# Attention with a mixture of experts on one core: the weights' chunks and the routed rows' stores move from SyncE's DMA queue to ScalarE's

## The reference, cut to what matters

```
x = L0_attn_x                              # (2, 2048, 512), f32
xn = layernorm(x)
# attention: rmsnorm, ternary qkv weights, 16 heads of 32, chunks of 128 tokens
#   intra = (q k^T * decay mask) v ;  cross = q * decay * S ;  S = decay * S + k^T v
#   two rmsnorms of the result, ternary output projection
# ffn: router -> softmax -> top 2 of 8 experts, weights summed to one
#   routed = sum over the 2 experts of combine * (silu(x Wg) * (x Wu)) Wd      (256 wide)
#   shared = (silu(x Sg) * (x Su)) Sd                                           (1024 wide)
return x + attention(xn) + routed(xn) + shared(xn)
```

## Time and profile before

| | |
|---|---|
| median of 3 runs | 1262.44 us |
| the profiled execution | 1262.65 us |
| its span, first to last instruction | 1260.9 us |
| PE busy | 1200.6 us, 95% |
| DVE, ACT, POOL busy | 53%, 38%, 39% |
| mean granted TensorE clock | 0.992 |
| DMA moved | 217.4 MB, mean 172 GB/s |
| q1, the queue of SP | 180.03 MB |
| q10, the queue of ACT | 0.81 MB |

### The profile page before, as it was taken

How to read it: one execution, slowest core, us unless ns; L and a number is a source line. 1 busy time by engine, 2 the same in 40 slices (tenths; PEclk the granted TensorE clock), 3 DMA queues, 4 the chain that set the end, 5 groups by cost and what they waited for, 6 DMA issues and landing times. The chain is left out here.

```text
span 1260.9 us, 29255 instructions
## 1 busy us (share of the span) xinstructions
PE 1200.6 (95%) x10768; PEld 812.0 (64%) x10768; DVE 664.4 (53%) x1410; ACT 477.9 (38%) x1031; POOL 493.3 (39%) x432
## 2 busy tenths in 40 slices
PE   3899999999999779999999899999999999999998
PEld 3676677677677557777777444444444577777776
DVE  7998889898898578633333322222222233333333
ACT  6454555555555462322222233333333311111111
POOL 3366655665676210344410222222222044444443
PEclk9999999999999889999999999999999999999999
DMA  8388888788878674344432777788888544444443
GB/s 284 97 241 197 206 226 244 187 221 231 222 204 219 204 212 156 87 124 94 111 109 23 182 193 191 192 195 182 190 184 193 123 156 152 151 151 152 151 153 110
DMA packets 269373, 217.40 MB, mean 172 GB/s; under 512 B 196784, under 2 KB 203056, under 8 KB 269296
## 3 DMA queue, kind: packets, MB, share of 16 engines
q1 hardware_dynamic: 255344, 180.03, 54.3%
q0 software_dynamic: 12848, 35.47, 10.3%
q10 hardware_dynamic: 1104, 0.81, 0.2%
HBM read 115.97 MB, written 56.51 MB: 137 GB/s over the span
## 5 line engine op out<-in xcount | busy, mean ns | idle before, releaser
L596 PE MATMUL sc<-x,WG 128*128 128x256 f16 x3072 | 346.0, 273 | 0.3 <-PEq L2099 0.3
L596 PEld LDWEIGHTS sc<-x,WG 128*128 128x128 f16 x3072 | 300.6, 98 | 48.6 <-issue 0.8
L1609 PE MATMUL yp<-WD,work 128*128 128x512 f16 x768 | 176.2, 379 | 1.4 <-DVE work L2016 1.0
L1586 POOL DMA_INDIRECT raw<-xs_dram,slots x71 | 67.3, 948 | 280.2 <-DMA raw<-raw 127.0
L2011 DVE SCALAR_TENSOR_TENSOR work<-sc,up_inv,work 128x512 f32<-128x512 f32 x63 | 47.3, 750 | 244.4 <-ACT work L1844 244.2
L1844 ACT ACTIVATE work<-sc,gate_inv 128x512 f32<-128x512 f32 x63 | 43.3, 687 | 303.4 <-PE sc L596 299.9
L1609 PEld LDWEIGHTS yp<-WD,work 128*128 128x128 f16 x768 | 74.8, 98 | 79.8 <-DVE work L2016 2.3
L864 PE MATMUL ring<-WG 128*128 128x256 f16 x1024 | 120.9, 275 | 2.0 <-PEq L264 2.0
L2084 POOL DMA_INDIRECT raw<-y_dram,gidx x64 | 63.6, 994 | 130.3 <-DVE gidx L2000 113.2
L2221 DVE TENSOR_TENSOR work<-rat,work 128x256 f16<-128x256 f32 x71 | 30.1, 424 | 155.5 <-ACT work L2198 155.5
L1602 PE MATMUL sc<-WG,raw 128*128 x432 | 104.8, 379 | 6.6 <-PEq L1620 3.4
(11 more groups left out here) (263 smaller groups left out, 1749.7 us busy)
## 6 DMA issues: line engine op xcount, KB each, us to landing
y_dram<-raw SPq DMA_DIRECT2D x71, 256.0 KB
WD<-in_L_attn_x SPq DMA_DIRECT2D x16, 512.0 KB, 4.5
work<-in_L_ffn_w_gate_up SPq DMA_DIRECT2D x16, 512.0 KB, 4.7
xs_dram<-WG SPq DMA_DIRECT2D x16, 512.0 KB, 3.7
xT_dram<-x SPq DMA_DIRECT2D x16, 512.0 KB, 2.7
WG<-in_L_attn_x SPq DMA_DIRECT2D x16, 512.0 KB, 5.4
x_dram<-WG SPq DMA_DIRECT2D x32, 256.0 KB, 2.1
x<-xT_dram SPq DMA_DIRECT2D x16, 512.0 KB, 7.5
```

Source lines behind the costliest of these rows:

```text
L596: ins = pe.matmul(gu[:, h, f * 2 * P:(f + 1) * 2 * P].rearrange("p (u t) -> p u t", u=2), w[:, kk, b, part * P:(part + 1) * P], x[:, :, a ...
L1586: pool.indirect_dma_start(out=xg[:, r % XG], out_offset=None, in_=xs_dram, in_offset=bass.IndirectOffsetOnAxis(ap=slots[:, r, 0:1], axis=0 ...
L1609: ins = pe.matmul(y[:], act_hl[a][:, f, :], w[:, f, b, :] if len(w.shape) == 4 else w[:, 0, f, b, :], start=(first and f == 0 and (a, b) = ...
```

## The change

`load_weights` goes from SP's step to ACT's, where it stands after `x_high(*nxt)` and before `take_oT(0, ...)`. It keeps its wait in other words: the count passed is the chunk's own, two higher, so `n - 1` there is `n + 1` here. In the routed block the store of a tile's result goes from SP to ACT, where it stands after the `ah` copy of the next tile. SP keeps its wait on `gu_full` and the transposes there, and no longer waits for `y_ready`.

```
                 if front:
                     turn_x(*after(q, par))
                     store_xs(*after(q, par))
-                if norm:
-                    sp.wait_ge(S["wmax_ready"], n + 1)
-                    load_weights(q + 1, par)
-                elif front:
+                if front and not norm:
                     load_group(sp, k, 1)
...
+            def load_weights(q, par):
+
+                n = 2 * q + par
+                act.wait_ge(S["wmax_ready"], n - 1)
+                for w, size, a in zip(flat, PART, START):
+                    act.dma_start(wraw[:, par, a:a + size], w[:, bass.ds(n * size, size)]).then_inc(wraw_in[par], 16)
...
                 x_high(*nxt)
+                if norm:
+                    load_weights(q + 1, par)
                 take_oT(0, q, par, st)
...
                     for r in range(SLOT_TILES):
                         if XH <= r + 3 < SLOT_TILES:
                             wait_apart(sp, S["gu_full"], r + 3 - XH + 1, S["sp_passed"])
                             turn(sp, r + 3, S["sp_passed"])
-                        store(r)
...
+                    rows = y_dram.rearrange("(r p) c -> r p c", p=P)
+
+                    def store(q, par):
+                        r = 2 * q + par
+                        act.wait_ge(S["y_ready"], r + 1)
+                        act.dma_start(at_step(rows, r), ysb[:, par]).then_inc(y_out[par], 16)
...
+                        last = (q, 0) if par == 1 else (q - 1, 1)
                         if not first:
-                            y_evac(*((q, 0) if par == 1 else (q - 1, 1)))
+                            y_evac(*last)
                         act.wait_ge(S["at_full"], r + 1)
                         act.activation(ah[:, par], at[par][:], ACT.Copy).then_inc(S["ah_ready"], 1)
+                        if not first:
+                            store(*last)
 
                     run_steps(act, step)
                     y_evac(SLOT_TILES // 2, 0)
+                    store(SLOT_TILES // 2, 0)
```

More of the change, by code:

```diff
@@ L764, in store_x1 @@
                 sp.dma_start(dst[:, u], x1[:, u]).then_inc(x1_out[u], 16)
[L766 to L769, removed]
             def store_xT(q, par):
@@ L2125, in _ @@
                 def _(sp):
-                    rows = y_dram.rearrange("(r p) c -> r p c", p=P)
                     load_tokens(sp, 1, 0, HALF)
-                    def store(r):
-                        sp.wait_ge(S["y_ready"], r + 1)
-                        sp.dma_start(rows[r], ysb[:, r % 2]).then_inc(y_out[r % 2], 16)
                     for r in range(SLOT_TILES):
```

## The result

The changed kernel takes 1296.33 us (median of 4 runs, 1293.96 to 1300.87) against 1262.31 us before (4 runs, 1260.25 to 1265.57). The ratio is 1.0264, with a 95% interval of 1.0232 to 1.0296: 2.6% slower, and outside the range of 1255 to 1277.

A forecast was written before the change was run, and what follows sets the result against it. PE was taken to bound the kernel, with attention's steps sensitive to when `load_xl` lands. 1262.65 + 5.5 (attention's loop) - 3.3 (routed rows) = 1264.9 us, given as 1265, range 1255 to 1277.

The forecast's parts named there:

- The rule for the step: Attention's loop: a wait of `row_stats` for `load_xl` is free up to 0.66 us; beyond that it lengthens the step one for one.
- one lateness and not a sum: Attention: `turn_h` is delayed too, but gets no price of its own; PE's lateness from it and DVE is one by `proj(0)`.
- D: Attention: the delay in `load_xl`'s landing in every step from the earlier weights' chunk, taken as 0.7 us.
- the prediction's own sum: Attention's thirteen steps: waits lengthened by D give 13.5 us of excess where there were 8.05, so +5.5 us.
- The chunk moves about 8 us earlier: Attention: the weights' chunk is asked at 204.1 to 206.3, just ahead of `load_xl`, delaying it; net +5.5 us in the loop.
- my nearest row: Attention: `load_xr`, asked 0.5 us behind the chunk, lands after 5.4 us against 4.5 for `load_xl`, 0.9 us more.
- The 16% of idle share: Attention before `load_xl` lands: DMAs 84% busy; if the chunk fits into the idle 16%, D is 0.
- the chunk and everything else goes ahead: Attention, slower rival: all of it goes ahead of `load_xl`, D = 1.43, +15.0 us in the loop, 1274.4 us; chance 0.24.
- The highest bound: Attention: `load_xl` is delayed by the chunk's whole transfer time, 3.7 us, which gives +44 us.
- The wait for `wmax_ready` is ... past: ACT in attention: this wait is for a chunk read in the step before, so it costs 0.
- The relief of `turn_y`: Attention's loop: `turn_y` no longer lands late behind the weights' chunk and `load_xr`; 2.52 us counted as gained.
- The routed rows: Routed block: SP no longer waits for `y_ready`, so PE's two waits for a transpose should go, -3.3 us.

## Why the prediction was wrong

**The rule for the step** (a wait of `row_stats` over 0.66 us counts one for one) was right: 39.1 us by it, 39.2 measured. That `turn_h` and DVE are one lateness and not a sum was right for the changed kernel nearly to the end: PE waited 8.8 us for `turn_h` in three of the first steps, and the sum over the steps is explained without them, if by the luck of three errors that cancel. With DVE's wait shortened it was no longer free (26.4 us of such waits in the kernel with `row_stats` later). With D = 2.67 in the prediction's own sum the loop comes out at +31.1 us, as measured, so nothing but D was wrong in it.

**"The chunk moves about 8 us earlier", the term D** is the step that failed. It was taken as 0.7 us and was 2.67; times 13 this is 25.6 us of the 31 missed (1296.3 - 1265); 3.8 are step 0, below, and the median is 2.3 over the profiled execution. Three things in it were wrong.
- *The order.* I let ACT ask when `x_high` ends, about 204.1 in the step of the earlier trace rows, behind `turn_h` at 203.48. ACT's first issue comes 0.1 us after the first `x_high` starts (220.97 and 221.06), while its ACTIVATEs still run. So three of the chunk's four DMAs are asked ahead of `turn_h`. How much of D the order makes is not shown: held until `x_high` was done, 1.2 us later and behind the first transpose, the kernel was no faster.
- *Who is hit.* I counted the bytes ahead of `load_xl`'s landing and took the time of its ask as fixed. Per step the time from the start of `turn_h` to the ask of `load_xl` went from 3.96 to 6.07 us, from the ask to `row_stats` from 4.68 to 5.11 (means of thirteen steps). Of the delay of 2.5 us, 2.1 are SP held in the issue of two transposes. `load_xr`, my nearest row, stood right behind the chunk with no transpose between them, and could not show this.
- *The rate.* I used 322 GB/s, the rate of the earlier trace rows, from a stretch in which no transpose was issued. In the 13 us from the chunk's ask to `load_xl`'s landing the DMAs were busy throughout (1.08) and moved 267 GB/s; over the thirteen steps it is 273 on average, between 228 and 299. The 16% of idle share before was no spare room of 322 GB/s.

The rival "the chunk and everything else goes ahead" was right in kind, and its 1.43 us still too small, for the last two reasons. The highest bound, the chunk's whole time, 3.7 us, did hold D, but nothing between 1.43 and it was in the range.

**"The wait for `wmax_ready` is ... past"** failed in step 0: there ACT waits with the prologue's chunk not yet read, its four issues run from 58.39 to 60.87, and `take_oT(0)` follows late. Two rows of ACT's timeline:

```profile
59.88 0.99 ACTq L1128 DMA_DIRECT2D work<-in_L_ffn_w_sh_down  x1
60.92 0.60 ACT L1042 ACTIVATE WG<-ring 128x512 f32<-128x512 f32 x1 [4.98 <-issue]
```

It costs 3.8 us once, of which 3.3 are PE's wait for this eviction; the first stretch at the lower clock, at 63.3, lies behind it. The first `proj` is at 77.11 with a quarter of the bytes as well, but at 73.17 where ACT asks after `take_oT(1)`. In the other steps the issues cost nothing, as predicted: `take_oT(0)` starts at PE's release.

**The relief of `turn_y`** was right: PE waited 4.2 us for `yT` in the loop before, has no such wait in it after, and the 2.52 us are gone in the agreement of rule and excess. **The routed rows** were right: -3.3 us predicted, no wait for a transpose after, and about -3.7 us for that part alone, known to some 3 us.

Sum: 1262.65 + 31.1 (loop) + 3.8 (step 0) - 3.3 (routed) = 1294.3, beside 1293.99 of the profiled execution.

**Queue or moment.** Shown: the early moment costs 2.4% from SP and 2.6% from ACT. In the versions with a late transfer it is each time one in flight with the chunk (`turn_h` and `load_xl`, `turn_x`, or `turn_y(1)`); after `o_square(1)` it is ACT's own time for the issues. The Trainium skill ("DMA: Bandwidth & Descriptors", section "Issuing engines are not separate DMA queues") says that a second issuer saves only its sequencer's time; these runs agree: no version with the weights on ACT was faster than its like on SP (1.0264 beside 1.0244 early, 1.0004 beside 0.9965 late in the step), and the best one has them on SP. Open: how much the second queue adds by itself. In the early pair the transposes were held 2.1 us longer than before beside ACT's queue and 1.1 us longer behind the chunk on SP, but there the chunk was also 1 us further ahead of them. The other pair, ACT before `take_kv(1)` and SP behind `turn_y(1)`, is 0.4% apart with intervals that overlap, and their moments differ. Open too is why a transpose's issue takes longer beside a plain load; the runs show that it does, not what holds it.

## What to carry to other kernels

A transfer that is moved to another engine's queue also moves in time, and it loses its place in the one list that kept it behind the urgent ones; read the new moment from where that engine's DMA issues can start at the earliest, not from where its work before them ends. When a large load comes to lie beside transposes, price the issuing engine's held time and everything behind it in its list, and not only the bytes. If a load has slack, look for the stretch in which no transfer is waited for, and leave it on the queue whose order guarantees that stretch.

## What was unexpected of the hardware

- SP's issue of a DMA transpose (`turn_h`) took 1.24 us in the median before the change; with the weights in flight on the other queue it took 1.84 us and up to 4.0 (two of them 2.89 us and 5.04 in the mean). Its landing went from 3.1 to 6.2 us.
- ACT's DMA issues ran beside its own ACTIVATEs: the first started 0.1 us after the start of an ACTIVATE of 0.62 us that stands ahead of it. Two ACTIVATEs and four issues took 2.06 us from start to end (220.97 to 223.03).
- The effect of the bytes was not linear: a quarter, a half and the whole chunk delayed `load_xl` by 0.08, 0.64 and 2.67 us per step, each known to 0.6; from a half to the whole the delay grew by more than three times that from a quarter to a half, for twice the bytes.
- The rate with the DMAs fully busy was not one number: 322 GB/s in the earlier trace rows, 267 in the stretch in which the chunk, four transposes, a store and `load_xl` were asked. From SP alone, with the same transfers asked in one queue, it was 290 in one step (240.0 to 251.5).
- What a late transfer costs can bring the lower clock with it: after the change PE waited 3.3 us until 61.6 and the clock was at its lower level from 63.3 to 66.7; in the kernel with `row_stats` later this came in six of thirteen steps.
